# Rounding of an fp8-style MLP: the subtraction on VectorE instead of GpSimd, a bf16 magic number, and all loops written out

## The reference

```python
def _triangle(x, ...):            # layers 0, 1 and 3, up to names, biases and the mask
    xn = layer_norm(x)
    left, right = (xn @ Wa) * sigmoid(xn @ Wga), (xn @ Wb) * sigmoid(xn @ Wgb)
    out = einsum('bikc,bjkc->bijc', left, right)
    return (layer_norm(out) @ Wo) * sigmoid(xn @ Wgo)

def _quantize_rowwise(x):
    scale = clip(max(abs(x), axis=-1), 1e-12, None) / 448.0
    return (x / scale).astype(float8_e4m3fn), scale

def _mlp(x, ln_w, ln_b, w1, w2):  # layer 2; _fp8_linear quantises both operands by rows
    h = layer_norm(x) * ln_w + ln_b
    a, b = split(_fp8_linear(h, w1), 2)          # 64 -> 512 -> two of 256
    return _fp8_linear(relu(a) * b, w2)          # 256 -> 64
```

## Time and profile before

| | |
|---|---|
| median of 3 runs | 2160.91 us (2160.28 to 2163.39) |
| the profiled execution | 2166.4 us, its span 2164.6 us |
| busy: PE matmul, weight load | 1628.8 us (75%), 1021.9 us (47%) |
| busy: DVE, ACT, POOL | 1762.3 us (81%), 1277.8 us (59%), 1367.9 us (63%) |
| instructions | 39427 |
| mean granted TensorE clock | 0.855 of 2.4 GHz |

### The profile page before, as it was taken

How to read it: one execution, slowest core, us unless ns; L and a number is a source line. 1 busy time by engine, 2 the same in 40 slices (tenths; PEclk the granted TensorE clock), 3 DMA queues, 4 the chain that set the end, 5 groups by cost and what they waited for, 6 DMA issues and landing times.

```text
span 2164.6 us, 39427 instructions
## 1 busy us (share of the span) xinstructions
PE 1628.8 (75%) x9710; PEld 1021.9 (47%) x9744; DVE 1762.3 (81%) x4086; ACT 1277.8 (59%) x2583; POOL 1367.9 (63%) x880
## 2 busy tenths in 40 slices
PE   5389999898799998991111588787778659999865
PEld 1156667564566675650111133333333336666654
DVE  6799952696999625978999699999999869993388
ACT  2156642696455425974666476666666537773398
POOL 7288820585878304868899347777777877760154
PEclk8689999899899998995555558888888789999979
DMA  5034333576344335762111001111111124333367
GB/s 216 10 88 106 97 72 75 154 200 192 86 99 104 71 73 137 220 189 59 39 43 45 0 10 40 39 39 39 39 37 34 45 69 106 97 80 81 92 228 257
DMA packets 314267, 200.63 MB, mean 93 GB/s; under 512 B 248992, under 2 KB 249312, under 8 KB 314208
## 3 DMA queue, kind: packets, MB, share of 16 engines
q1 hardware_dynamic: 201888, 171.65, 27.1%
q10 hardware_dynamic: 112320, 28.32, 5.8%
HBM read 114.97 MB, written 66.06 MB: 84 GB/s over the span
## 4 chain that ended last, share of the span: by engine, by line
DVE 34%; issue 31%; PE 12%; ACT 10%; POOL 5%; DMA 4%; DVEq 2%; ACTq 1%; SPq 0%; POOLq 0%
DVE pairs L874 5%; ACT work L960 4%; DVE work L724 4%; DMA gate_dram<-work 4%; DVE tok L844 4%; PE ps L1072 3%; DVE stats L697 3%; DVE tok L838 3%; PE ps L1111 3%; PE ps L1165 2%; DVE pairs L751 2%; PE ps L1101 2%; DVE pairs L829 2%; DVE pairs L868 1%; ACT pairs L960 1%
## 5 line engine op out<-in xcount | busy, mean ns | idle before, releaser
L481 POOL TENSOR_TENSOR ln_s<-ln_s,half_power 128x8 f32<-128x8 f32 x252 | 418.2, 1660 | 411.0 <-DVE ln_s L706 358.4
L1072 PE MATMUL ps<-work,ones 128*128 128x512 f32 x504 | 289.2, 690 | 49.1 <-POOL work L497 21.4
L1111 PE MATMUL ps<-work 128*128 128x384 f32 x864 | 319.9, 493 | 2.6 <-ACT work L946 2.6
L971 ACT ACTIVATE work<-ps 128x768 f32<-128x768 f32 x216 | 175.3, 811 | 198.8 <-DMA gate_dram<-work 150.3
L960 ACT ACTIVATE work<-pairs,ln_s 128x64 f32 (+1 forms) x648 | 263.9, 501 | 23.4 <-DVE ln_s L713 23.3
L522 POOL TENSOR_TENSOR work<-pairs 128x1024 bf16<-128x1024 f32 x72 | 203.3, 2843 | 48.2 <-DVE pairs L874 48.2
L1116 PE MATMUL ps<-work 128*128 128x256 f32 x864 | 223.7, 382 | 0.0
L724 DVE TENSOR_SCALAR work<-work,ln_s 128x64 f32<-128x64 f32 x468 | 207.1, 508 | 0.0
L766 DVE COPY pairs<-ps 128x576 f32 (+1 forms) x48 | 36.4, 758 | 207.0 <-PE ps L1135 207.0
L1116 PEld LDWEIGHTS ps<-work 128*128 128x128 f32 x864 | 165.6, 192 | 69.8 <-DVE pairs L751 3.9
L1101 PE MATMUL ps<-ident,work 128*128 128x128 f32 x864 | 143.7, 292 | 70.6 <-DVE work L724 56.1
(11 more groups left out here) (134 smaller groups left out, 3613.7 us busy)
## 6 DMA issues: line engine op xcount, KB each, us to landing
work<-x_mid SPq DMA_DIRECT2D x144, 256.0 KB, 2.6
gate_dram<-work ACTq DMA_DIRECT2D x108, 256.0 KB, 3.0
work<-gate_dram SPq DMA_DIRECT2D x108, 256.0 KB, 3.0
work<-in_x_in SPq DMA_DIRECT2D x72, 256.0 KB, 2.7
work<-pairs SPq DMA_DIRECT2D x192, 96.0 KB, 2.2
work<-x_nat SPq DMA_DIRECT2D x144, 128.0 KB, 2.9
x_mid<-work SPq DMA_DIRECT2D x72, 256.0 KB, 2.0
x_nat<-work SPq DMA_DIRECT2D x72, 128.0 KB, 2.3
```

The lines of the kernel that those rows point to most:

```text
L481: pool.tensor_tensor(ln_s[:, b, RSTD, :], ln_s[:, b, VAR, :], half_power[:, 0:U], ALU.pow)\
L971: act.activation(sig[:, b, :].rearrange("p (k g) -> p k g", k=PAIRS)[:, 2 * half:2 * half + 2, :], ps[:, bank:bank + 2, 0:GATES], ACT.Sigm ...
L1072: last = pe.matmul(ps[:, bank, :], ones[:], src[:, b, :], start=first, stop=end, skip_group_check=True)
L1111: last = pe.matmul(ps[:, GATE_BANK[half] + k, 0:GATES], xnT[:, b, (2 * half + k) * P:(2 * half + k + 1) * P], wpair[:, VALUES:VALUES + GAT ...
```

## The change

1. `h_round` and `hidden_round` move from POOL to DVE. In the first pass the rounding comes right after `h_add`; in the second the adds and roundings are spread between the products, the second rounding being the last instruction of an iteration.
2. The magic numbers `h_magic` and `magic` are bf16 instead of f32. ACT writes them and DVE takes their maximum in place, as before in an instruction of its own.
3. The row maxima are one instruction of 2048 elements instead of two of 1024.
4. The square for the group sums of layer 3 moves from POOL to ACT, after the first absolute.
5. `turns = 0` in `pipeline`: every loop of every engine is written out.

```diff
@@ pipeline
-    turns = max(t0 + n - max(leads) - start, 0) // turn
+    turns = 0
@@ buffers
-        h_norm, h_pre, h_act, h_scaled, h_magic, h_added = (part(wide, 1024 * k, ROW) for k in range(6))
+        h_norm, h_pre, h_act, h_scaled, h_added = (part(wide, 1024 * k, ROW) for k in range(5))
+        h_magic = part(wide, 5120, ROW // 2).bitcast(BF16)
-        scaled, magic = (part(wide, 8192 + 4096 * k, U * HID) for k in range(2))
+        scaled = part(wide, 8192, U * HID)
+        magic = part(wide, 12288, U * HID // 2).bitcast(BF16)
@@ POOL, layer 2
                                     (3, lambda t, b: token_rstd(l, 0, t, b)),
-                                    (1, h_bias),
-                                    (-1, h_round)])
+                                    (1, h_bias)])
                     pipeline(pool, [(-6, lambda t, b: update_mlp(l, t, b)),
-                                    (-6, lambda t, b: shift_new(l, t, b)),
-                                    (-3, lambda t, b: hidden_round(0, t, b)),
-                                    (-3, lambda t, b: hidden_round(1, t, b)),
-                                    (-6, lambda t, b: square_new(l, t, b))])
+                                    (-6, lambda t, b: shift_new(l, t, b))])
@@ DVE
             def h_add(t, b):
                 dve.wait_ge(hadd_step, t + 1)
-                wait_free(dve, hq_ready, t - 1)
+            def h_round(t, b):
+                dve.wait_ge(hadd_ready, t + 1)
+                wait_free(dve, qT_psum, t - 1)
+                dve.tensor_tensor(q_in[:, b, :], h_added[:, b, :], h_magic[:, b, :], ALU.subtract).then_inc(hq_ready, 1)
-            def hidden_amax(half, t, b, r):
...
+            def hidden_amax(t, b, r):
+                dve.wait_ge(acc_used, PAIRS * (t + 1))
+                dve.tensor_reduce(tok[:, 3, :], hidden_rows(r), AX.X, ALU.max, apply_absolute_value=True).then_inc(hid_step, 1)
+            def hidden_round(half, t, b):
+                part_ = slice(half * HALF * HID, (half + 1) * HALF * HID)
+                dve.wait_ge(hid_added, 2 * t + half + 1)
+                if half == 0:
+                    wait_free(dve, hqT_psum, 2 * (t - 1))
+                dve.tensor_tensor(q_hid[:, b, part_], scaled[:, b, part_], magic[:, b, part_], ALU.subtract).then_inc(hid_q, 1)
@@ DVE, layer 2
                                    (-1, h_add),
+                                   (-1, h_round),
                                    (5, lambda t, b, r: centre(l, t, b, r), RING)])
                     pipeline(dve, [pair(0), (-6, lambda t, b: mlp_update(l, t, b)), (-3, hidden_max),
-                                   pair(1), add(0), add(1), (-1, square_sx),
-                                   pair(2), amax(0), amax(1), (-1, amax_of_product),
-                                   pair(3), (-1, hidden_row_scale), (-1, hidden_inverse), (-1, hidden_rescale)])
+                                   pair(1), (-1, square_sx), (-1, hidden_amax, RING), add(0), (-1, amax_of_product),
+                                   pair(2), round_(0), (-1, hidden_row_scale), add(1), (-1, hidden_inverse),
+                                   pair(3), (-1, hidden_rescale), round_(1)])
@@ ACT, layer 2, second pass
-                                   pair(2), evacuate(0), absolute(0),
+                                   pair(2), evacuate(0), absolute(0), (-6, lambda t, b: square(sum_base(l) + t, b)),
```

More of the change, by code:

```diff
@@ L509, in h_bias @@
                     .then_inc(h_ready, 1)
-            def h_round(t, b):
-                pool.wait_ge(hadd_ready, t + 1)
-                wait_free(pool, qT_psum, t - 1)
-                pool.tensor_tensor(q_in[:, b, :], h_added[:, b, :], h_magic[:, b, :], ALU.subtract)\
-                    .then_inc(hq_ready, 1)
-            def hidden_round(half, t, b):
-                part_ = slice(half * HALF * HID, (half + 1) * HALF * HID)
-                pool.wait_ge(hid_added, 2 * t + half + 1)
-                if half == 0:
-                    wait_free(pool, hqT_psum, 2 * (t - 1))
-                pool.tensor_tensor(q_hid[:, b, part_], scaled[:, b, part_], magic[:, b, part_], ALU.subtract).then_inc(hid_q, 1)
             for l in range(layers):
@@ L838, in square_sx @@
                 dve.tensor_tensor(tok[:, 4, :], tile_row(sx_all, t), tile_row(sx_all, t), ALU.mult).then_inc(hid_step, 1)
-            def hidden_amax(half, t, b, r):
-                if half == 0:
-                    dve.wait_ge(acc_used, PAIRS * (t + 1))
-                us = slice(HALF * half, HALF * half + HALF)
-                last = dve.tensor_reduce(tok[:, 3, us], hidden_rows(r)[:, us, :], AX.X, ALU.max, apply_absolute_value=True)
-                if half:
-                    last.then_inc(hid_step, 1)
+            def hidden_amax(t, b, r):
+                dve.wait_ge(acc_used, PAIRS * (t + 1))
+                dve.tensor_reduce(tok[:, 3, :], hidden_rows(r), AX.X, ALU.max, apply_absolute_value=True).then_inc(hid_step, 1)
             def amax_of_product(t, b):
@@ L908, in _ @@
                     pair = lambda pp: (0, lambda t, b, r: hidden_product(pp, t, b, r), RING)
[L909 removed]
+                    round_ = lambda half: (-3, lambda t, b: hidden_round(half, t, b))
                     add = lambda half: (-3, lambda t, b: hidden_add(half, t, b))
                     pipeline(dve, [pair(0), (-6, lambda t, b: mlp_update(l, t, b)), (-3, hidden_max),
[L912 to L914 removed]
+                                   pair(1), (-1, square_sx), (-1, hidden_amax, RING), add(0), (-1, amax_of_product),
+                                   pair(2), round_(0), (-1, hidden_row_scale), add(1), (-1, hidden_inverse),
+                                   pair(3), (-1, hidden_rescale), round_(1)])
         @block.scalar
```

6 lines of the change are left out of this document (removed).

## The result

| | before | after |
|---|---|---|
| median of 4 runs | 2160.6 us (2158.8 to 2163.4) | 2080.6 us (2063.3 to 2090.7) |
| the profiled execution | 2166.4 us, span 2164.6 us | 2083.8 us, span 2082.0 us |
| instructions | 39427 | 31474 |

The ratio is 0.962 (95% interval 0.955 to 0.969). The forecast was 2097 us.

The account below looks back on a forecast made before the run. DVE was taken as the bound in both passes of layer 2, slowed by meeting POOL. Terms -46 - 14 - 2 + 8 - 4 - 6 = -64 us took 2160.9 to 2097 us, range 2060 to 2140.

Parts of the forecast that it names:

- DVE work of a second-pass tile: Layer 2's second pass, steady tiles: DVE's work falls from 13.7 to 11.35 us a tile, before waits.
- The instruction with an f32 and a bf16 input: Second pass on DVE: two added subtractions of 1024 elements at 1.13 us each, +2.3 us a tile; adds also 1.13.
- ACT's wait: Second pass: DVE waits 0.5 to 0.6 us a tile for relu(1), as ACT's scalings wait for DVE's last rounding.
- The shift's collision: Second pass: L838 may meet POOL's shift and wait 1.0 us; a quarter taken, giving 12.2 us a tile.
- Drain -14, fill -2: Second pass's ends: draining falls from 48 to 32 us, taken as -14; three iterations of filling give -2.
- First pass +0.25 a tile: Layer 2's first pass: DVE's rounding costs more than is given back, +0.25 us a tile, +8 us over 36 tiles.
- Outgoing passes -6: Layers 0 and 1: less register work before POOL's L481 gives 12 us, halved to -6 (0 to -14).
- Elsewhere the branch is hidden: 0: Written-out loops outside opening sums and outgoing passes gain 0, since TensorE, ACT or the POOL lock sets the pace.
- Rival A: L838 meets the shift in every tile, 13.0 us a tile, first pass +0.5 a tile: 2136 us; chance 0.15.
- D: Rival with more gain: L838 always ahead, mixed instructions cheaper, first pass gains, PE the floor: about 2047 us; chance 0.10.
- B (clock): Rival, slower: TensorE's granted clock is low for 0.85 of the second pass, 15.1 us a tile: 2187 us; chance 0.05.
- C (code): Rival, slower: written-out code needs 66 packets on q8; at 1.2 us stall each, 2176 us; chance 0.04.

Follow-up runs that it names:

- h_round_pool: The changed kernel with the first pass's rounding (512 elements) put back on POOL: 2046.8 us, ratio 0.947.
- magic_f32: The changed kernel with the second pass's magic number in f32 again: 2080.4 us, ratio 0.964.
- adds_first: The changed kernel with both second-pass adds back ahead of the square of sx and the long reduce: 2112.4 us, ratio 0.976.
- hidden_round_pool: The changed kernel with the second pass's roundings put back on POOL: 2086.5 us, ratio 0.965.
- square_on_pool: The changed kernel with the square for layer 3's group sums back on POOL, behind the shift: 2070.3 us, ratio 0.956.
- loops_out: The kernel before with every loop of every engine written out and nothing else: 2122.8 us, ratio 0.981.
- both_rounds_pool: The changed kernel with the roundings of both passes put back on POOL: 2062.6 us, ratio 0.954.

## Why the prediction was right, and where it wasn't

The forecast was 16 us above the median. Its steps in order:

- **DVE work of a second-pass tile, 11.35 us.** A tile of `h_round_pool`, whose second pass is the same, takes 11.38 (1445.38 to 1456.76) with a wait of 0.52 in it, so the work is about 10.9 and the sum was 0.5 too high. The square of sx went from 2.32 to 0.16 as forecast, and the adds and the maximum came out as forecast too.
- **The instruction with an f32 and a bf16 input.** Taken at 1.13 of pitch. It takes 1.21 to 1.22 and the next starts 1.13 later. The Trainium skill, "VectorE: DVE Perf Modes", section "What auto-detection actually checks", wants all tensors at 16 bits for the doubled rate, and these rows agree. The maximum, with one input and all bf16, takes 0.68 for 2048 elements, and 1.22 in f32 (forecast about 0.7).
- **ACT's wait, 0.5 to 0.6.** 0.51 in every tile of `h_round_pool` and in the long tiles of the changed kernel. But what it covers was not costed: `magic_f32` shows that the 0.54 us saved on the maximum goes into this wait, and what is gained in the end is that the square finds POOL's update over. A saving ahead of a wait is at best part of a gain, and the sum counted both the saving and the wait.
- **The shift's collision, a quarter of 1.0 us.** The square never meets the shift. It comes so early that it can meet the end of the update before it: not in a long tile (0.16), and for 0.26 us in a short one of the changed kernel (0.42 at 1445.38; POOL's update L489 runs from 1444.13 to 1445.78). Alone, update and shift take 1.27 and 1.26 us (1659.99 and 1661.35, in the drain), not 1.0. What I had left out is a further wait of 0.8 us in each second tile, which comes with the lower clock level. 12.2 was forecast, 11.92 measured, and 11.38 where the clock stays up. Steady part: -55 us instead of -46.
- **The attribution.** The second largest saving, the adds after the long reduce, was put at -1.5 a tile; undoing it cost 0.95. The largest, -2.2 on L838, was put down to the rounding L522 leaving POOL. That is enough: in `adds_first`, with DVE's old order, the square takes 0.15. But it isn't needed: in `hidden_round_pool`, with the rounding on POOL and the new order, the square takes 0.16 (1459.67), and two other 8-element instructions pay the 2.9 us instead. So the order decides which instruction waits. The -0.25 on L850 was put down to POOL's square leaving; with that square back on POOL (`square_on_pool`) it still takes 0.15 in the new order.
- **Two SBUF inputs.** The prediction said that DVE instructions which read one SBUF tile keep their time beside POOL. It holds for the long reduce but not for L842 (1.64 us), and the maximum L847, which reads one tile, holds up POOL's update. The sum has no term for either.
- **Drain -14, fill -2.** Measured -9.4 and -1.2. From the update that follows the last product to the last sums it is 38.6 us (1633.5 to 1672.1), where the sum had 32. About half of the rest is in iterations 36 to 38, 25.7 us instead of 22.3: the step took their adds and roundings at 1.13, but with no long reduce ahead of them one add waits for POOL's update and one rounding for its shift, and iterations 37 and 38 take 8.0 us each. The other half is behind the last rounding, 12.9 us instead of 9.6, where DVE waits 4.73 and 2.69 us for PE's outputs. The rows of one tile:

```profile
1652.54 2.17 DVE L853 TENSOR_TENSOR pairs<-pairs 128x1024 f32<-128x1024 bf16 x1
1654.75 2.17 DVE L860 TENSOR_TENSOR work<-pairs 128x1024 bf16<-128x1024 f32 x1
1656.84 1.21 DVE L853 TENSOR_TENSOR pairs<-pairs 128x1024 f32<-128x1024 bf16 x1
1658.09 1.23 DVE L860 TENSOR_TENSOR work<-pairs 128x1024 bf16<-128x1024 f32 x1
```

- **First pass +0.25 a tile.** 6.88 against 6.44, +0.44; +11.6 us in the stage. The 1.75 us instruction, 1.07 of it waiting, stayed, on the rescale instead of the add. The given-back part was too large: L724's counterpart L703 takes 0.30, not 0.16, and L692 now takes 0.66 (its counterpart L713 0.43), since it ends with POOL's scaling L475, which starts earlier.
- **Opening sums -4.** -4.9.
- **Outgoing passes -6.** Nothing. POOL's idle time before its root did fall from 0.33 to 0.18, but its shift then waits 0.26 to 0.39 for PE's sums. The step halved the gain for this; it had to be taken whole.
- **"Elsewhere the branch is hidden: 0".** This is the step that failed, by 30 us. It was right that POOL's lock sets the pace of an incoming pass, and wrong that register work is therefore hidden: 0.2 us of it on DVE decides whether one or two L724 come behind POOL's scaling, 0.24 us a tile.
- **Rival A (half the gain)** and **D** stayed away. Of the signs of being wrong, the product's wait for ACT came in part: 1.6 us in all in a long tile, though none of the three is above 0.80. **B (clock)**: the granted clock did not fall under 0.8 in the second pass, but the mechanism is there: 27 us between the runs at 0.849 and 0.871. **C (code)**: the page of the changed kernel shows

```profile
q8 instruction: 78, 1.28, 0.3%
q14 instruction: 89, 0.73, 0.1%
```

that is 78 packets on q8 instead of 22, more than the 66 I had put, and `loops_out` has the same packets and is 40 us faster than the kernel before. The most that could be put down to the written-out code is the 0.3 to 1.4 us by which its three product stages got longer. The Trainium skill, "Runtime: NRT & Kernel Launch", section "Instruction fetch mechanics", says that sequential fetching is hidden; these runs agree.

That the number came within 16 us is partly luck. By the profiles -82.7 us was measured for -64: the 30 us of the incoming passes and 8.5 in the steady second pass had been left out, and 14 us counted for the drain, the first pass and the outgoing passes did not come. The cause was also partly different from mine: the move of the subtraction, which names the change, costs 2 to 18 us, depending on the clock (`both_rounds_pool`, 18 by the medians), because its first half loses more than its second half gains; the rest of the change brings 98.

## What to carry to other kernels

Where two engines share a lock on SBUF, ask first which instructions stand beside which, and move the two-input ones next to work that doesn't take the lock: the order was worth more here than the engine. A loop's register work can count even where another engine's lock sets the pace: 0.2 us of it put one more instruction behind the lock in every tile. Look for starts that are further apart than the instruction before is long, and for what stands just ahead of the other engine's instruction. Of what is saved ahead of a wait, nothing is gained until the wait is gone.

## What the runs showed of the hardware

- An 8-element instruction with one SBUF input also waits for POOL: L842 of `hidden_round_pool`, 1.64 us instead of 0.16, ends with POOL's rounding. The long reduce (2.28) keeps its time beside POOL.
- DVE's maximum in place, one SBUF input, holds up POOL in turn. POOL's update of 512 elements takes 1.27 us alone, 1.65 behind the bf16 maximum and 2.19 behind the f32 one, and ends 1.13 to 1.14 us after the maximum does (1457.03 after 1455.90; 1456.51 after 1455.37). In the kernel before the same 2.19 stands behind the same f32 maximum.
- The mean granted clock differs between runs of one kernel by 0.02, and where PE is busy for 92% of the time that is worth 1.3%.
- The same idle time of PE, 1.73 us, was followed at once by the lower clock level in a tile of the changed kernel (1452.95) and by the upper in one of `h_round_pool` (1443.71).
